# The value products of two chunks of keys in one place of the second attention's order of work

## What is computed

```python
x = x + _L0_attn_ref(_layernorm(x), ...)   # 16 heads of 128, rope, window of 128
x = x + _L0_ffn_ref(_layernorm(x), ...)    # 16 experts, 6 of them for each token, and a shared one
x = x + _L1_attn_ref(_layernorm(x), Wq, Wk, Wv, Wo, bo)
x = x + _L1_ffn_ref(_layernorm(x), w1, b1, w2, b2)   # weights rounded to three values
```

```python
q = (x @ Wq).reshape(b, s, NUM_HEADS, HEAD_DIM)      # 16 heads of 16 features; k and v alike
scores = jnp.einsum('bqhd,bkhd->bhqk', q, k) * SCALE
p = jax.nn.softmax(scores, axis=-1)
o = jnp.einsum('bhqk,bkhd->bqhd', p, v).reshape(b, s, e)
return o @ Wo + bo
```

## Time and profile before

| | us |
|---|---|
| runs | 1470.15, 1472.76, 1472.74 |
| median | 1472.74 |
| the profiled execution | 1465.43, span 1463.7 |
| TensorE matmul busy | 1379.4 (94%) |
| TensorE weight loads busy | 1048.3 (72%) |
| VectorE busy | 1083.8 (74%) |
| ScalarE busy | 730.2 (50%) |
| GpSimd busy | 469.0 (32%) |
| chain that ended last | PE 68%, DVE 15%, POOL 5%, issue 5% |

### The profile page before, as it was taken

The page is one execution under the profiler, slowest core; times in us unless marked ns, Lnnn a source line. Parts: engine busy times, 40 slices in busy tenths (PEclk is TensorE's granted clock), DMA queues, the critical chain, the costliest instruction groups (busy, mean ns, idle before and its releaser), DMA issues.

```text
span 1463.7 us, 24351 instructions
## 1 busy us (share of the span) xinstructions
PE 1379.4 (94%) x7518; PEld 1048.3 (72%) x7518; DVE 1083.8 (74%) x2509; ACT 730.2 (50%) x1883; POOL 469.0 (32%) x725
## 2 busy tenths in 40 slices
PE   4899999999999999799999999999987999999898
PEld 3689889988998898577777777777763344444476
DVE  6999999989999998477555455455546787877454
ACT  4555565556555655244332232232323676767575
POOL 5766657765776665000000000001002131412100
PEclk9899999999999999899999999999995899999999
DMA  5200000000000000332000000000123333232001
GB/s 183 77 29 1 2 2 2 2 3 1 1 1 1 2 1 2 83 97 86 23 0 1 1 0 0 0 0 13 47 74 129 101 102 115 100 125 91 1 15 43
DMA packets 31714, 57.00 MB, mean 39 GB/s; under 512 B 3316, under 2 KB 11508, under 8 KB 31316
## 3 DMA queue, kind: packets, MB, share of 16 engines
q1 hardware_dynamic: 31204, 54.95, 11.6%
q0 software_dynamic: 400, 0.71, 0.3%
HBM read 41.69 MB, written 15.73 MB: 39 GB/s over the span
## 4 chain that ended last, share of the span: by engine, by line
PE 68%; DVE 15%; POOL 5%; issue 5%; ACT 2%; DMA 2%; SPq 1%; DVEq 0%; ACTq 0%; POOLq 0%
PE ps L1332 13%; PE ps L1334 12%; PE ps L1333 12%; PE ps L1601 5%; PE ps L1640 5%; PE ps L1418 4%; PE ps L1376 3%; DVE ssum L727 2%; DVE qkn L716 2%; POOL rope L469 2%; PE ps L1732 2%; POOL rms L467 2%; PE ps L1482 2%; DVE nmax L707 2%; PE ps L1754 1%
## 5 line engine op out<-in xcount | busy, mean ns | idle before, releaser
L930 DVE TENSOR_REDUCE nm<-ps 128x1 f32<-128x512 f32 x256 | 166.2, 685 | 68.4 <-PE ps L1601 67.8
L1332 PE MATMUL ps<-xnT_lo,w1moe_hi 128*128 128x512 f32 x400 | 177.4, 444 | 4.0 <-DVE w2moe_lo L878 3.8
L1249 ACT ACTIVATE pT<-ps 128x512 f32<-128x512 f32 x256 | 143.2, 598 | 66.2 <-PE ps L1614 64.4
L428 POOL TENSOR_TENSOR ln_rs<-ln_ve,minus_half 128x4 f32<-128x4 f32 x12 | 13.6, 1132 | 488.0 <-DVE ln_ve L590 488.0
L1333 PE MATMUL ps<-xnT_hi,w1moe_lo 128*128 128x512 f32 x400 | 160.5, 401 | 0.0
L1334 PE MATMUL ps<-xnT_hi,w1moe_hi 128*128 128x512 f32 x400 | 159.9, 400 | 0.0
L1162 ACT ACTIVATE moe_act_hi<-sg 128x512 fp32r<-128x512 f32 x100 | 63.4, 634 | 192.7 <-DVE sg L855 192.7
L845 DVE TENSOR_TENSOR sg<-ps,sg 128x512 f32<-128x512 f32 x100 | 69.1, 691 | 94.9 <-ACT sg L1182 94.9
L469 POOL TENSOR_TENSOR rope<-rope 128x384 f32<-128x384 f32 x128 | 132.8, 1037 | 0.0
L1332 PE MATMUL ps<-wqkv_lo,xnT_hi 128*128 128x512 f32 x256 | 126.5, 494 | 6.6 <-DVE wqkv_lo L643 3.4
L1601 PE MATMUL ps<-kst,qst 64*128 64x512 f32 x256 | 107.5, 494 | 17.1 <-DMA kst<-copies 15.3
(11 more groups left out here) (212 smaller groups left out, 3706.7 us busy)
## 6 DMA issues: line engine op xcount, KB each, us to landing
copies<-qk_hi SPq DMA_DIRECT2D x32, 256.0 KB
qst<-copies SPq DMA_DIRECT2D x32, 256.0 KB, 2.6
kst<-copies SPq DMA_DIRECT2D x32, 256.0 KB, 3.0
yT<-in_w1moe SPq DMA_DIRECT2D x25, 256.0 KB, 2.6
x_res<-in_wqkv SPq DMA_DIRECT2D x8, 512.0 KB, 4.5
copies<-qk_lo SPq DMA_DIRECT2D x16, 256.0 KB
w_in<-in_w2moe SPq DMA_DIRECT2D x25, 128.0 KB, 2.7
x_res<-in_wo SPq DMA_DIRECT2D x4, 512.0 KB, 3.8
```

Source lines behind the costliest of these rows:

```text
L930: V.tensor_reduce(nm1[:, n % 2, t, col:col + 1], ps[:, 1 + s1_slot(p), :], AX.X, ALU.max, negate=True).then_inc(s1_max, 1)
L1249: A(pT1[:, u % 2, 2 * (m % 2) + h, c, :], ps[:, 4 + e % 2, :], ACT.Exp, scale=SCALE1).then_inc(p1_ready, 1)
L1332: MM(out, left[0], right[1], start=first, stop=False)
```

## The change

In an odd step the value products of chunks 0 and 1 are issued together behind place 6 (before: 0 behind place 5, 1 behind place 7). In the even step that follows, those of chunks 2 and 3 are issued together behind place 2 (before: 2 behind place 1, 3 behind place 3). The waits for the exponents are made once a place, for the later of its two chunks. The instructions and their number, their order among themselves, the banks and the other engines' programs stay as they were.

```diff
--- before.py
+++ after.py
@@ -1626,21 +1626,23 @@
                             ins = T(ps[:, 7, t * P:(t + 1) * P], nm1[:, m % 2, t, :], ident[:])
                         ins.then_inc(m_turned, 1)
                     u = (n - 3) // 2 if n % 2 else (n - 4) // 2
-                    if valid(u) and i in ((5, 7) if n % 2 else (1, 3)):
-
-                        c = (i - 5) // 2 if n % 2 else 2 + i // 2
-                        if c == 0:
+                    if valid(u) and i == (6 if n % 2 else 2):
+
+                        if n % 2:
                             if old or u >= 1:
                                 pe.wait_ge(oT1_kept, kq + u)
                             if u == 0:
                                 pe.wait_ge(v_kept, 2 * b + 2)
-                        pe.wait_ge(p1_ready, (kb + 2 * u + 1) * 2 * TT + TT + c + 1)
-                        for h in range(4):
-                            col = (4 * (u % (PAIRS // 2)) + h) * VW
-                            ins = MM(ps[VW * h:VW * (h + 1), 6, :], v1[:, c, col:col + VW],
-                                     pT1[:, u % 2, h, c, :], start=c == 0, stop=c == TT - 1,
-                                     tile_position=(0, VW * h), skip_group_check=True)
-                        if c == TT - 1:
+                            pe.wait_ge(p1_ready, (kb + 2 * u + 1) * 2 * TT + TT + 2)
+                        else:
+                            pe.wait_ge(p1_ready, (kb + 2 * u + 2) * 2 * TT)
+                        for c in ((0, 1) if n % 2 else (2, 3)):
+                            for h in range(4):
+                                col = (4 * (u % (PAIRS // 2)) + h) * VW
+                                ins = MM(ps[VW * h:VW * (h + 1), 6, :], v1[:, c, col:col + VW],
+                                         pT1[:, u % 2, h, c, :], start=c == 0, stop=c == TT - 1,
+                                         tile_position=(0, VW * h), skip_group_check=True)
+                        if not n % 2:
                             ins.then_inc(o1_ready, 1)
                     if n % 2 == 0 and valid((n - 4) // 2) and i == 6:
```

## The result

| | us |
|---|---|
| before, median (4 runs) | 1471.45 (1469.24 to 1472.76) |
| changed, median (4 runs) | 1492.17 (1490.16 to 1493.23) |
| ratio, 95% interval | 1.0141 (1.0122 to 1.0160) |
| profiled execution, before and after | 1465.43 and 1492.52 (spans 1463.7 and 1490.8) |

A forecast was written before the change was run, and what follows sets the result against it. TensorE's queue, in its written order, sets the time. Two full batches 12.3, the last 5.2, the first 2.2 and the tail 0 make 19.7 us slower, on the 1472.74 median 1492.4 us; range of 8 in 10, 1478 to 1500.

The forecast's parts named there:

- The double place: Place with two chunks of value products together: claimed 1.86 us instead of 2.00, saving 0.14 us each.
- Three pairs in a row: Row and key score pairs with nothing between: third key score starts 1.22 us after the first, a wait of 0.56.
- Even steps 0.52 us: Places 3, 4 and 5 stand in a row, so the projection behind place 5 starts later: loss 0.52 us.
- Even steps without a projection: Places 4, 5, 6 stood in a row before too, so the change was costed at 0.
- Steps 1 and 5: Odd steps with a projection at place 3 whose copies hold ScalarE; maxima predicted later, loss 1.36 us each.
- step 3: Odd step with turns at places 2, 4, 6 and 0; key score 6 hardly waits, loss 0.2 us.
- step 5 of the last batch: Odd step of the last batch, which has no projections in steps 4 and 5; maxima later by 0.97 us.
- Step 7: Odd step with one ScalarE copy less; maxima predicted at 1238.48 against 1237.33, loss 1.15 us.
- The first batch: Value products only from step 3 on, steps 3 and 7 largely at half clock; loss 2.2 us in all.
- the tail: Steps 0 to 2 without new scores, ending in value products that already stand together: costed at 0.
- the second rival: Odd steps' waits partly absorbed by emptier VectorE and ScalarE queues: loss only 10.7 us, 1483.4 us; chance 22%.
- The third rival, the clock: New waits in front of double places drop TensorE to half clock: 17 us more, 1509.5 us; chance 8%.

The follow-up runs named there:

- odd_only: Kernel before with only chunks 0 and 1 put together behind place 6 of odd steps, even steps unchanged; 1483.24 us against 1467.75, ratio 1.0096.

## Why the prediction was right

The median came at 1492.17 us, where I had written 1492.4. That it fits to 0.3 us is luck: with a fourth run the median of before came down by 1.3 us, to 1471.45, and the loss was 20.7 us, not 19.7. The mechanism is what held. Point by point:

- *The double place takes 1.86 us.* It does, at every full-clock place (1267.90 to 1269.76).
- *Three pairs in a row cost 1.22 us from the first key score to the third.* Measured 1.21 to 1.22 in even steps and behind the odd double places but for step 7 (below), and 1.00 with the shorter exponent. Here the prediction rested on one natural example, which had the whole mechanism in it.
- *Even steps 0.52 us.* Mis-sized: 0.59 to 0.63. I took 0.33 us from the pair of place 2 to the double place, what a pair takes beside another pair. Here it stands alone, between the turn and the double place, and takes 0.43 (1267.47 to 1267.90). Those 0.1 us, for 12 places, are 1.2 us. The trace of before had this price too, behind a value place and ahead of a turn:

```profile
1266.57 0.50 PE L1614 MATMUL ps<-qsm,kst 64*128 64x512 f32 x1
1267.00 0.66 PE L1571 MATMUL ps<-ident,xn 128*128 128x128 f32 x4
```

- *Even steps without a projection 0.* Batch 0 step 6 and batch 3 step 4 measured 0.12 each.
- *Steps 1 and 5 1.36, step 3 0.2, step 5 of the last batch 0.97.* Measured 1.33 to 1.36, 0.20 and 0.95.
- *Step 7 1.15.* Mis-sized: 1.28, 1.21 and 1.23 in batches 1 to 3. In batches 1 and 2 another wait stood in front there, shown here in batch 1. The last row score of a batch doesn't go to the next bank of the ring of three but to bank 2, so the one of place 1 of the next batch needs the maximum taken just before:

```profile
1247.51 0.49 PE L1601 MATMUL ps<-kst,qst 64*128 64x512 f32 x1
...
1248.79 0.50 PE L1601 MATMUL ps<-kst,qst 64*128 64x512 f32 x1 [0.54 <-DVE nm L930]
1248.88 0.49 PE L1614 MATMUL ps<-qsm,kst 64*128 64x512 f32 x1
1249.30 0.66 PE L1626 MATMUL ps<-ident,nm 128*128 128x128 f32 x4
```

  A wait in the code (`s1_slot`) that I had read and not walked. The row score comes so late that the key score of place 1 starts 1.36 us after that of place 7 (place 7's row score is at 1247.51), not 1.22. It cost only 0.14 because the exponent would have held it nearly as long.
- *The first batch 2.2 in all, the tail 0.* The steps at half clock were the unsure term: up to batch 1 step 0 the ledger has 3.84 us in one trace and 2.67 in the other. The tail, from the last turn to the first projection behind it, cost 1.3 and 0.2.
- *None of it hides behind another wait.* So it was: the second rival, that the odd steps' loss is partly absorbed, is contradicted by a ledger that rises by 6.54 us in batch 1, 6.56 in batch 2 and 5.68 in the last, where I had 6.15, 6.15 and 5.2.
- The sum: 19.7 predicted, 22.6 and 21.5 in the traces, 20.7 in the medians. Terms of 1 us and more were too small or left out (even steps, the first batch, the tail), all to the same side.
- The third rival, the clock, didn't come in the middle of the stage: every window of 10 us from 1180 to 1390 us has the full clock in the changed kernel. But it is not refuted: `odd_only`, with fewer of the new waits, fell to half in step 5 of the last batch (granted clock 0.50 from 1363 to 1364 us), for 1.2 us.

By the rule of the Trainium skill, page "TensorEngine Tiling (Array Packing)", section "Tiling Modes", a change of tiling mode drains TensorE. The trace agrees: with half the changes two chunks take 1.86 us and not 2.00, 0.14 us for each change and back. No run here is faster as a whole for it; the new waits cost more.

## What to carry to other kernels

In a queue that runs in its written order, work of one kind is also the cover for the waits of another. Before two pieces are put together to save their fixed cost, look at what stands between them and on both sides afterwards, and walk the shortest producer's ring (here two banks, 1.22 us for two steps) against TensorE's 0.33 us a step. The trace of before mostly has a spot where the future order occurs already; take the price from there. And a wait that looks like the last (here for VectorE) may hide another just behind it: taking away the wait alone gave 0.2%, with the filler moved as well 0.5%.

## What the runs showed of the hardware

Three things I had not expected. A pair of scores that stands alone between other work takes 0.43 us in the queue, whether a turn (1267.47 to 1267.90, changed kernel) or a value place (1266.57 to 1267.00, before) stands ahead of it; beside another pair it takes 0.33 to 0.34. So a pair's price depends on what stands on both sides of it. The same program meets the clock at different points of time: the projection of 1.99 us took 3.62 in one of two executions of the changed kernel, at a granted clock of half, in a sparse stretch at the end of the stage. And in `odd_only` the clock fell to half at 1362.4 us in a dense stretch, where the waits of TensorE that the trace shows in the 5 us before were 0.25, 0.28 and 0.27 us.
